# Gated cross-attention with a two-of-eight expert layer: earlier second tile, later weight loads, subtractions on GpSimd, another order of the stacked keys

## The chip, the cores and the metric

The kernel runs on one core of a Trainium2 chip. The metric is the device time of one execution in microseconds; lower is better. The kernel before was timed three times: 310.95, 310.99 and 312.33 us, median 310.99 us. In the text PE is TensorE (PEld its weight loads), DVE is VectorE, ACT is ScalarE, POOL is GpSimd and SP is SyncE.

## The reference

The inputs are `x` (32 batches of 128 tokens by 128 features), `ctx_768` (32 batches of 77 context tokens by 96 features), two gains and the weights. All is float32.

```
q = (layer_norm(layernorm(x)) @ Wq + bq)        16 heads of 8 features
k, v = (layer_norm(ctx) @ Wk + bk), (... @ Wv + bv)
y = softmax(q k^T / sqrt(8)) v                  per batch and head, 128 x 77 scores
x = x + tanh(g_xattn) * y
z = layernorm(x);  logits = z @ w_router;  two experts of eight by top_k, softmax over the two
x = x + tanh(g_ffn) * sum over both of prob * (relu(z @ w1[e])^2 @ w2[e])
```

## The kernel before, in words

**Tiles, steps, slots.** Four batches make a tile, so there are eight tiles (0 to 7). The program is a pipeline of steps i = -2 to 9, and each step has four slots j = 0 to 3. In slot (i, j) each engine works on several batches at once: `near[k]` is the batch k places away from batch j of tile i. A slot has the first two blocks of scores of `near[3]`, the last two of `near[2]`, the turned scores and exponentials of `near[0]` and `near[1]`, the product with the values and the head normalisation of `near[-1]`, and the turn and routing of `near[-2]`. Beside this one slot prepares a later tile (normalise, transpose, project to keys, queries, values) and two experts of an earlier tile run in each slot from (1, 2) on. Each engine's instructions are written in one fixed order, and semaphores join the engines.

**Scores.** The sixteen heads go in four blocks c of four heads. Queries and keys are split into a high part and a low part in fp32r. They are stacked in `qs` and `ks`, 96 rows of three terms with 32 rows each, and 8 rows for the negative maxima. `scores` (L507) makes 128 tokens by 4 x 78 scores in one matmul, so that DVE can take the row maxima (`maximum`, L1043). These maxima are transposed (L513), copied (L753) and sent by DMA into `qs` (L347). `scoresT` (L528) then makes the scores turned with the maximum already subtracted, and ACT takes the exponential (L822).

**How `ks` and `qs` are filled.** ACT writes the high part of the projection (L770, L778) and DVE the low part (L1004, L1013). Then DMAs move 32 partitions of `k_hi` or `k_lo` to 8 partitions of `ks`: twelve DMAs of 39 KB per tile, four on SP (L327) and eight on POOL (L1416, L1421). In `ks` a head's 4 x 78 keys of the four batches lie in one run of 312 numbers. Queries go in three DMAs of 256 KB, all on SP (L341). Tiles 0 and 1 don't do this for queries: `project_query_rows` (L482) makes the stacked rows by four matmuls with `wq_rows`, ACT copies them (L789) and DVE subtracts (L1023).

**Banks.** Short products share two banks of PSUM, `ab_0` and `ab_1`, in a fixed turn (`AB_USES`, `ab_sequence`). A matmul may write a bank only after the one before it has been read out.

**The post chain.** For each batch: product with the values (L551), copy of the heads (L808), transpose (L560), then on DVE reciprocal, product, sum, statistics (L1062 to L1082), then the reciprocal root on POOL (L1388, L1390), the normalisation on DVE (L1088) and the turn on PE (L566) with its two copies on ACT (L814, L815). `low_x` (L1095) on DVE gives the low part of the turned input for the experts. `output` is L596, `hidden` is L589 to L591, `gated` is L1160, `square` is L827.

**Start.** Tile 1 is normalised in slot (-1, 3) and projected in slot (0, 0). Both expert weights are loaded by ACT at (-1, 0) (L842), split or scaled by ACT at (0, 1) to (1, 0) (L849, L853), and the low part of `w1` is made by DVE (L1033). Memsets of `ks` and `vs` for the second parity run on POOL. `keep_on` (L462) issues matmuls whose results nobody reads.

## Time and profile before

| | |
|---|---|
| median of three runs | 310.99 us |
| the profiled execution | 310.82 us, its span 309.0 us, granted clock 0.997 |
| PE busy | 286.2 us, 93% of the span |
| DVE busy | 231.6 us, 75% |
| ACT busy | 179.2 us, 58% |
| POOL busy | 112.4 us, 36% |
| DMA moved | 30.83 MB |

The span is the time from the first to the last instruction on the core; the time of the execution is 1.8 us more. An engine's busy share is an average over the start, the steady middle and the end, which have different limits. A busy PE includes the latency of each matmul, so 93% does not mean that its array works 93% of the time.

### The profile page before, as it was taken

To read this page: it belongs to the slowest core of one execution; us is meant where nothing else is said; L and a number is where in the kernel's file an instruction comes from. 1 tells how busy PE (TensorE), PEld (TensorE's weight loads), DVE (VectorE), ACT (ScalarE), POOL (GpSimd) and SP (SyncE) were. 2 spreads that over 40 slices of the span, in tenths; PEclk is the share of its full clock that TensorE was granted. 3 is DMA by queue.
4 is the path that set the end of the run, shared out by engine and by line. 5 is a ranking of instruction groups with operands and counts; after the bars stand their busy time and mean duration, and the time that the engine had idled before them with its cause. 6 is when DMAs were issued, how large, how long until landed. Compare 5 with 4: busy or idle time off the path is not lost.

```text
span 309.0 us, 7855 instructions
## 1 busy us (share of the span) xinstructions
PE 286.2 (93%) x2837; PEld 235.2 (76%) x2837; DVE 231.6 (75%) x934; ACT 179.2 (58%) x412; POOL 112.4 (36%) x211
## 2 busy tenths in 40 slices
PE   7887889799999999999999999999999999989894
PEld 5555467577878888888888888888788787878784
DVE  7887687788688977888698868886668666646765
ACT  0533656555665676565656665567656555655573
POOL 6594543473156323652166116422612211221110
PEclk9999999999999999999999999999999999999998
DMA  3362301193529363934575275727391620070011
GB/s 71 96 160 59 64 6 51 35 134 110 224 45 118 74 180 139 130 79 127 188 118 101 72 243 76 94 60 249 64 108 35 204 87 3 6 304 6 0 36 34
DMA packets 19078, 30.83 MB, mean 100 GB/s; under 512 B 5321, under 2 KB 11626, under 8 KB 19040
## 3 DMA queue, kind: packets, MB, share of 16 engines
q1 hardware_dynamic: 12144, 22.35, 30.5%
q0 software_dynamic: 3408, 6.61, 9.3%
q10 hardware_dynamic: 3488, 1.38, 1.7%
q8 instruction: 22, 0.36, 0.5%
q14 instruction: 16, 0.13, 0.2%
HBM read 18.94 MB, written 2.21 MB: 68 GB/s over the span
## 4 chain that ended last, share of the span: by engine, by line
PE 56%; DVE 25%; issue 8%; ACT 4%; ACTq 2%; POOL 2%; DMA 1%; SPq 1%; DVEq 0%; POOLq 0%
PE y L596 14%; PE c L551 9%; PE ab L507 6%; DVE u L1160 4%; PE s L528 3%; DVE negm L1043 3%; PE ab L574 3%; PE ab L566 2%; PE h L589 2%; PE h L591 2%; PE h L590 2%; PE ab L457 2%; DVE o L1066 2%; DVE m_parts L1050 2%; DVE st L1078 2%
## 5 line engine op out<-in xcount | busy, mean ns | idle before, releaser
L822 ACT ACTIVATE p<-s 77x512 f32<-77x512 f32 x128 | 74.4, 583 | 18.7 <-PE s L528 18.5
L1043 DVE TENSOR_REDUCE negm<-ab 128x4 f32<-128x308 f32 x128 | 60.4, 474 | 32.6 <-PE ab L507 30.6
L528 PEld LDWEIGHTS s<-qs,ks 104*77 104x77 f32 x512 | 54.0, 148 | 11.6 <-issue 3.7
L596 PE MATMUL y<-w2s,hs 128*128 128x128 f32 x448 | 60.4, 279 | 2.6 <-ACT hs L827 2.6
L528 PE MATMUL s<-qs,ks 104*77 104x128 f32 x512 | 59.2, 238 | 0.6 <-ACT p L822 0.6
L596 PEld LDWEIGHTS y<-w2s,hs 128*128 128x128 f32 x448 | 55.4, 193 | 4.6 <-ACT hs L827 3.7
L1388 POOL TENSOR_SCALAR rs<-mv 128x1 f32<-128x1 f32 x32 | 7.3, 228 | 131.6 <-DVE mv L1082 131.6
L507 PE MATMUL ab<-ks,qs 96*128 96x312 f32 x128 | 49.4, 387 | 4.8 <-DVE negm L1043 1.6
L827 ACT ACTIVATE hs<-u 128x512 f32<-128x512 f32 x56 | 34.9, 624 | 13.6 <-DVE u L1160 13.6
L1160 DVE SCALAR_TENSOR_TENSOR u<-h,gb 128x512 f32<-128x512 f32 x56 | 37.8, 677 | 1.9 <-PE h L591 1.5
L551 PE MATMUL c<-p,vs 77*32 77x128 f32 x1024 | 34.6, 276 | 0.0
L507 PEld LDWEIGHTS ab<-ks,qs 96*128 96x128 f32 x128 | 24.4, 191 | 9.8 <-DVE negm L1043 3.9
L589 PE MATMUL h<-x_hi,w_lo 128*128 128x512 f32 x64 | 31.4, 490 | 0.4 <-DVE top L1104 0.4
L808 ACT ACTIVATE oT<-c 128x256 f32<-128x256 f32 x32 | 12.3, 384 | 32.8 <-PE c L551 32.8
L551 PEld LDWEIGHTS c<-p,vs 77*32 77x32 f32 x1024 | 26.0, 109 | 4.8 <-issue 4.5
L591 PE MATMUL h<-x_hi,w_hi 128*128 128x512 f32 x64 | 25.2, 395 | 0.0
L590 PE MATMUL h<-x_lo,w_hi 128*128 128x512 f32 x64 | 25.2, 394 | 0.0
L1416 POOL DMA_DIRECT2D ks<-k_lo x32 | 18.2, 575 | 16.0 <-issue 8.9
L753 ACT ACTIVATE mT<-ab 32x128 fp32r<-32x128 f32 x32 | 8.4, 263 | 21.8 <-PE ab L513 21.8
L1390 POOL TENSOR_TENSOR rs<-rs,neg_half 128x1 f32<-128x1 f32 x32 | 18.3, 572 | 2.7
L1088 DVE TENSOR_SCALAR xn<-x,mv,rs 128x128 f32<-128x128 f32 x32 | 11.5, 361 | 9.3 <-POOL rs L1390 8.8
L1381 POOL TENSOR_TENSOR nrm<-nrm,neg_half 77x4 f32<-77x4 f32 (+1 forms) x16 | 17.4, 1086 | 1.3
(128 smaller groups left out, 500.6 us busy)
## 6 DMA issues: line engine op xcount, KB each, us to landing
gb<-gates_scratch SPq DMA_DIRECT2D x14, 768.0 KB, 5.7
gb<-gates_scratch SPq DMA_DIRECT2D x14, 256.0 KB, 3.5
qs<-q_hi SPq DMA_DIRECT2D x12, 256.0 KB, 7.6
out_dram<-y_out POOLq DMA_DIRECT2D x7, 256.0 KB, 6.4
x_sb<-in_x_dram POOLq DMA_DIRECT2D x6, 256.0 KB, 3.5
qs<-q_lo SPq DMA_DIRECT2D x6, 256.0 KB, 9.3
ks<-k_hi SPq DMA_DIRECT2D x34, 39.0 KB
ks<-k_lo POOLq DMA_DIRECT2D x32, 39.0 KB, 3.2
```

The costliest lines, as they stand in the source:

```text
L507: nc.tensor.matmul(p[:, 0:J * NP].rearrange("t (i n) -> t i n", n=NP), qs[0:QR, par, c, T * j:T * j + T], ks[0:QR, par, c, :, NP * j:NP * ...
L528: mm = nc.tensor.matmul(p[0:N, T * i:T * i + T], ks[:, par, c, i, NP * j:NP * j + N], qs[:, par, c, T * j:T * j + T], start=True, stop=True)
L551: mm = nc.tensor.matmul(bank_c[VT * i:VT * i + VT, r:r + T], vs[:, par, j, NC * i + c, :], p32[:, m % LR, T * i:T * i + T], start=(c == 0) ...
L589: nc.tensor.matmul(p[:, :], w1_lo[:, e, :], x_hi[:, par, :], start=True, stop=False)
L590: nc.tensor.matmul(p[:, :], w1_hi[:, e, :], x_lo[:, par, :], start=False, stop=False)
L591: nc.tensor.matmul(p[:, :], w1_hi[:, e, :], x_hi[:, par, :], start=False, stop=True).then_inc(h_ready, 1)
L596: mm = nc.tensor.matmul(bank_y[:, D * b:D * b + D], hs[:, e % 2, T * b:T * b + T], w2s[:, e, :], start=(e == 0 and b == 0), stop=(e == E - ...
L822: nc.scalar.activation(p32[:, m % LR, :], src, ACT.Exp).then_inc(p_done, 1)
L827: nc.scalar.activation(hs[:, e % 2, :], u[:, e % 2, :], ACT.Square).then_inc(hs_done, 1)
L1043: nc.vector.tensor_reduce(negm[:, :, c], bank_ab[bank][:, 0:J * NP].rearrange("t (i n) -> t i n", n=NP)[:, :, 0:N], AX.X, ALU.max, negate= ...
L1160: nc.vector.scalar_tensor_tensor(out=u[:, e % 2, :], in0=bank_h[e % 2][:, :], scalar=0.0, in1=gb[:, par, e, :], op0=ALU.max, op1=ALU.mult) ...
L1390: nc.gpsimd.tensor_tensor(rs2[:, 1:2], rs2[:, 0:1], neg_half[:, 0:1], ALU.pow).then_inc(post_p, 1)
```

## The change

Five things are changed together.

- **Order of the stacked keys.** `ks` is now `[row, parity, block, batch, head, 78]` instead of `[row, parity, block, head, batch x 78]`. The matmul of L507 reads one run of 312 numbers instead of four runs of 78. Each DMA into `ks` now writes runs of 78 numbers (312 bytes) where it wrote runs of 312 numbers (1,248 bytes).
- **Tile 1 earlier.** Its normalisation and projections are done in slots (-1, 1), (-1, 2) and (-1, 3). Its queries go the way of all later tiles: one projection, high and low part, DMAs (two on ACT, one on POOL). A table `SIDE` gives nine early uses (value projection of tile 0, and what tiles 1 and 2 need) a bank of their own out of four banks that are idle then.
- **Weights.** `w1` is loaded at (-1, 1) and split by ACT at (-1, 2); `w2` is loaded at (0, 2) and scaled at (1, 0) and (1, 1).
- **Low parts by POOL.** `low_x` of all tiles but the last and the low part of `w1` (in eight pieces) are done by POOL.
- **Order and place of smaller things.** The product with the values stands first on PE in slots (0, 2) to (1, 1). Zeroing of `vs` and part of `ks` is done by ACT (a copy with scale 0) instead of DVE and POOL. Some DMA issues go from ACT or POOL to SP or back. DVE and POOL orders around (0, 0) to (0, 2) differ in detail.

```diff
-AB_MOVED = [(("k", 0), ("ctxT", 0)), (("ctxT", 1), ("mT1", 0)), (("xT", 1), ("s1b2", 0)), (("k", 1), ("s1d2", 0))]
+AB_MOVED = [(("k", 0), ("ctxT", 0))]
+SIDE = {("v", 0): (5, 1), ("ctxT", 1): (2, 1), ("xT", 1): (3, 1), ("k", 1): (4, 1), ("q", 1): (2, 2),
+        ("ctxT", 2): (2, 3), ("xT", 2): (3, 2), ("k", 2): (4, 2), ("q", 2): (2, 4)}
...
-        ks = sb("ks", [MR, 2, NC, J, G * NP], F32R)
+        ks = sb("ks", [MR, 2, NC, G, J, NP], F32R)
...
-        bank_ab = [ps("ab_0"), ps("ab_1")]
+        bank_ab = [ps("ab_0"), ps("ab_1"), bank_h[0], bank_h[1], bank_y, bank_c]
...
-                turned = third if j == (3 if i == -1 else 2) else None
-                made = (1, 1) if (i, j) == (0, 0) else third if j == 3 and i != -1 else None
+                turned = third if j == 2 and i != -1 else None
+                made = third if j == 3 and i != -1 else None
...
-            return 2 if s == 0 else J
+            return {0: 0, 1: J - 1}.get(s, J)
...
-                        if term == 2 and i < k_shared(s):
+                        if term == 2 and (i < k_shared(s) or (s == 0 and i > 0)):
                             continue
                         r = QROWS * term + HD * i
-                        sp.dma_start(ks[r:r + HD, par, :, i, :].bitcast(F32),
-                                     k_hi[QROWS * i:QROWS * i + QROWS].rearrange("p b n -> p (b n)").bitcast(F32))\
+                        sp.dma_start(ks[r:r + HD, par, :, :, i, :].rearrange("p c b n -> p (c b) n").bitcast(F32),
+                                     k_hi[QROWS * i:QROWS * i + QROWS].bitcast(F32))\
                             .then_inc(k_stacked[par], 16)
 
...
+                    if term == 1 and s == 2:
+                        continue
...
+            for i in range(J // 2, J):
+                with nc.allow_non_contiguous_dma(reason="short vectors"):
+                    sp.dma_start(vec[QROWS * i:QROWS * i + QROWS, BQ:BQ + 1],
+                                 bq[QROWS * i:QROWS * i + QROWS].rearrange("(g d o) -> d g o", d=HD,
+                                                                           o=1)).then_inc(bq_in, 16)
+            sp.dma_start(ctx_sb[:, 1], ctx_v[1]).then_inc(ctx_first[1], 16)
+            sp.dma_start(x_sb[:, 1], x_v[1]).then_inc(x_first[1], 16)
...
+                    if (i, j) == (-1, 2):
+                        stack_k(1, 1)
+                    if (i, j) == (0, 0):
                         unit_rows(1)
...
-                nc.tensor.matmul(p[:, 0:J * NP].rearrange("t (i n) -> t i n", n=NP), qs[0:QR, par, c, T * j:T * j + T],
-                                 ks[0:QR, par, c, :, NP * j:NP * j + NP], start=True, stop=True).then_inc(ready, 1)
+                nc.tensor.matmul(p[:, 0:J * NP], qs[0:QR, par, c, T * j:T * j + T],
+                                 ks[0:QR, par, c, j].rearrange("p i n -> p (i n)"), start=True,
+                                 stop=True).then_inc(ready, 1)
...
-                    pe.wait_ge(experts_made, 4)
+                    pe.wait_ge(experts_made, 2)
+                    pe.wait_ge(experts_low, E)
                 if e == 0 and last(s):
-                    pe.wait_ge(late_d, at(LATE, G * s + G - 1, "x_lo"))
+                    pe.wait_ge(low_d, G)
+                if e == 0 and not last(s):
+                    pe.wait_ge(low_p, G * s + G)
...
-                    values_first = i == S - 1 and j != 1
+                    values_first = (i == S - 1 and j != 1) or (i == 0 and j > 1) or (i == 1 and j < 2)
...
+                    if (i, j) == (-1, 2):
+                        project_keys(1)
...
+                    if (i, j) == (-1, 3):
+                        project_queries(1)
...
+            def stack_first_k():
+
+                act.wait_ge(zeroed[0], ZEROED[0])
+                act.wait_ge(hi_k, 1)
+                for i in range(1, J):
+                    r = 2 * QROWS + HD * i
+                    act.dma_start(ks[r:r + HD, 0, :, :, i, :].rearrange("p c b n -> p (c b) n").bitcast(F32),
+                                  k_hi[QROWS * i:QROWS * i + QROWS].bitcast(F32))\
+                        .then_inc(k_stacked[0], 16)
...
+            def stack_q_rows(s, par):
+
+                if s >= 2:
+                    act.wait_ge(s2_ready, NC * G * (s - 1))
+                act.wait_ge(hi_q, s)
+                for term in ((0, 1) if s == 1 else (1,)):
+                    r = QROWS * term
+                    act.dma_start(qs[r:r + QROWS, par].bitcast(F32), q_hi[:, :].bitcast(F32))\
+                        .then_inc(q_stacked[par], 16)
+
+            def clear_some(par, some):
+
+                nc.scalar.activation(vs[:, par, some].rearrange("n b h v -> n (b h v)")
+                                     .rearrange("n (o k) -> n o k", k=D),
+                                     ident[0:N, :].rearrange("n (o k) -> n o k", o=1)
+                                     .broadcast_to([N, (some.stop - some.start) * H * VT // D, D]),
+                                     ACT.Copy, scale=0.0).then_inc(v_ones[par], 1)
+
...
+            act.wait_ge(const_made, 2)
+            for c, half in ((2, 1), (3, 0), (3, 1)):
+                nc.scalar.activation(ks[:, 1, c, 2 * half:2 * half + 2].rearrange("p b i n -> p (b i n)")
+                                     .rearrange("p (o k) -> p o k", k=MR),
+                                     ident[0:MR, 0:MR].rearrange("p (o k) -> p o k", o=1)
+                                     .broadcast_to([MR, 2 * G * NP // MR, MR]),
+                                     ACT.Copy, scale=0.0).then_inc(zeroed[1], 1)
...
-                    if (i, j) == (-1, 0):
-                        load_experts()
+                    if (i, j) == (-1, 1):
+                        clear_some(0, slice(0, G))
+                        evacuate_v(0, 0)
+                        evacuate_ctxT(1)
+                        load_experts(w1_in[:, :, :], w1.rearrange("e c d -> c e d"), first_in)
+                        clear_some(1, slice(0, G // 2))
+                        continue
+                    if (i, j) == (-1, 2):
+                        evacuate_k(1, 1)
+                        max_store(*near[2])
+                        evacuate_xT(1)
+                        prepare_experts(0)
+                        prepare_experts(1)
+                        continue
+                    if (i, j) == (-1, 3):
+                        max_store(*near[2])
+                        evacuate_q(1, 1)
+                        stack_q_rows(1, 1)
+                        clear_some(1, slice(G // 2, G))
+                        exponent(*near[1], 0)
+                        continue
...
+                    if made and made[0] == 2:
+                        stack_q_rows(*made)
...
+                    for part in PREPARING.get((i, j), ()):
+                        prepare_experts(part)
+                    if (i, j) == (0, 2):
+                        load_experts(w2s[:, :, :], w2.rearrange("e d c -> d e c"), experts_in)
...
-            def low_experts():
-
-                for part in range(2):
-                    dve.wait_ge(w1_split, part + 1)
-                    some = slice(E // 2 * part, E // 2 * part + E // 2)
-                    nc.vector.tensor_tensor(w1_lo[:, some, :], w1_in[:, some, :], w1_hi[:, some, :].bitcast(F32),
-                                            ALU.subtract).then_inc(experts_made, 1)
...
-                        clear_values(dve, nc.vector, 0)
...
+                    if (i, j) == (-1, 1):
+                        take(normalise_ctx(1, 1), 2)
+                    if (i, j) == (-1, 2):
+                        normed = normalise_x(1, 1)
+                        take(top_scores)
+                        take(normed)
+                        take(top_scores, 4)
+                        take(normed)
+                        take(tops_of(near[3]))
+                        take(low_keys(1, 1))
...
-                    if near[-2]:
+                    if near[-2] and last(near[-2][0]):
...
+            def low_x(s, par, j):
+
+                bank, k = ab(s, f"turn{j}")
+                pool.wait_ge(ab_taken[bank], k)
+                nc.gpsimd.tensor_tensor(x_lo[:, par, T * j:T * j + T], xT32[:, j % 2, :],
+                                        x_hi[:, par, T * j:T * j + T].bitcast(F32), ALU.subtract).then_inc(low_p, 1)
+
+            def low_expert(e):
+
+                pool.wait_ge(w1_split, 2 * e // E + 1)
+                nc.gpsimd.tensor_tensor(w1_lo[:, e, :], w1_in[:, e, :], w1_hi[:, e, :].bitcast(F32),
+                                        ALU.subtract).then_inc(experts_low, 1)
...
-                    pool.dma_start(ks[r:r + HD, par, :, i, :].bitcast(F32),
-                                   k_lo[QROWS * i:QROWS * i + QROWS].rearrange("p b n -> p (b n)").bitcast(F32))\
+                    pool.dma_start(ks[r:r + HD, par, :, :, i, :].rearrange("p c b n -> p (c b) n").bitcast(F32),
+                                   k_lo[QROWS * i:QROWS * i + QROWS].bitcast(F32))\
...
+            def stack_first_low_q():
+
+                bank, n = ab(1, "q")
+                pool.wait_ge(ab_taken[bank], n)
+                apart(pool)
+                pool.dma_start(qs[2 * QROWS:QR, 1].bitcast(F32), q_lo[:, :].bitcast(F32)).then_inc(q_lo_stacked, 16)
+
+            def zero_keys(c, half):
+
+                nc.gpsimd.memset(ks[:, 1, c, 2 * half:2 * half + 2].bitcast(F32), 0.0).then_inc(zeroed[1], 1)
...
+            zero_keys(0, 0)
+            zero_keys(0, 1)
+            zero_keys(1, 0)
...
             def step(i, par):
                 for j, near, nxt, third, turned, made, ffn in slots(i, par):
                     if (i, j) == (-1, 0):
-                        for c in range(NC):
-                            for half in range(2):
-                                nc.gpsimd.memset(ks[:, 1, c, 2 * half:2 * half + 2].bitcast(F32),
-                                                 0.0).then_inc(zeroed[1], 1)
                         norm_rstd(1, "ctx")
                         norm_rstd(1, "x")
-                    if (i, j) == (-1, 3):
-                        clear_values(pool, nc.gpsimd, 1)
+                        zero_keys(1, 1)
+                        zero_keys(2, 0)
+                        mark_values(pool, nc.gpsimd, 0)
+                    if (i, j) == (-1, 2):
+                        stack_low_k(1, 1)
                     if j == 1 and spread(i - 1):
                         gate_roots(i - 1)
                     if near[-1]:
                         rstd(*near[-1])
+                    if near[-2] and not last(near[-2][0]):
+                        low_x(*near[-2])
                     if j == (1 if i == 0 else 0) and i != -1 and third:
                         norm_rstd(third[0], "ctx")
                         norm_rstd(third[0], "x")
-                    if j == 0 and i > 0 and exists(i + 3):
+                    if j == (1 if i == 1 else 0) and i > 0 and exists(i + 3):
                         load(i + 3, 1 - par)
                     if made:
                         stack_low_k(*made)
-                    if (i, j) in ((-1, 3), (0, 1)):
-                        load(i + 3, 1 - par)
+                    if (i, j) == (0, 0):
+                        mark_values(pool, nc.gpsimd, 1)
+                        stack_first_low_q()
+                        load(2, 0)
+                    if (i, j) == (0, 1):
+                        load(3, 1)
+                    if (i, j) in ((0, 0), (0, 1), (0, 2), (1, 0)):
+                        part = ((0, 0), (0, 1), (0, 2), (1, 0)).index((i, j))
+                        low_expert(2 * part)
+                        low_expert(2 * part + 1)
                     if j == 2 and exists(i - 2) and not last(i - 2):
                         store(i - 2, par)
 
...
```

## Rows read from the trace of the kernel before

**Rows 1.** The page's first line, the span.
```profile
span 309.0 us, 7855 instructions
```

**Rows 2.** Busy time by stretch; columns end with clock, DMA share, GB/s.
```profile
35.84:74.69 38.85, 33.32 (x356) 25.81 (x359) 31.60 (x142) 22.66 (x56) 18.71 (x33) 1.00 0.33 61
90.00:122.75 32.75, 31.98 (x342) 27.24 (x343) 26.57 (x112) 20.70 (x49) 13.60 (x25) 1.00 0.60 127
```

**Rows 3.** Waits in 90:250: waiter, releaser, total us, times, longest.
```profile
PEld ab L566 <- DVE xn L1088: 3.7, 11, 0.5
...
PEld h L578 <- DVE gates L1149: 1.3, 5, 0.3
```

**Rows 4.** ACT and DVE in order of time, slots (0, 0) and (0, 1).
```profile
31.92 0.68 ACT L789 ACTIVATE qs<-c,bq_rows 96x512 fp32r<-96x512 f32 x1
...
35.08 1.06 ACT L822 ACTIVATE p<-s 77x512 f32<-77x512 f32 x2
...
35.48 1.41 DVE L1023 SCALAR_TENSOR_TENSOR qs<-h,bq_rows,qs 32x512 fp32r<-32x512 f32 x2
```

**Rows 5.** One turn of the post chain, slots (0, 2) to (0, 3).
```profile
43.92 0.33 PE L566 MATMUL ab<-ident,xn 128*128 128x128 f32 x1 [1.09 <-DVE xn L1088]
...
44.72 1.08 PE L551 MATMUL c<-p,vs 77*32 77x128 f32 x32
...
46.49 0.41 PE L560 MATMUL c<-ident,oT 128*128 128x128 f32 x2
...
50.03 0.34 DVE L1088 TENSOR_SCALAR xn<-x,mv,rs 128x128 f32<-128x128 f32 x1
...
50.90 0.30 PE L566 MATMUL ab<-ident,xn 128*128 128x128 f32 x1
```

**Rows 6.** DVE in order of time, slot (0, 3).
```profile
53.80 0.68 DVE L1033 TENSOR_TENSOR w_lo<-w_in,w_hi 128x512 fp32r<-128x512 f32 x1
54.40 0.47 DVE L1043 TENSOR_REDUCE negm<-ab 128x4 f32<-128x308 f32 x1
...
55.48 0.28 DVE L1095 TENSOR_TENSOR x_lo<-xT,x_hi 128x128 fp32r<-128x128 f32 x1
55.68 0.28 DVE L1073 TENSOR_TENSOR x<-x_sb,o 128x128 f32<-128x128 f32 x1
```

**Rows 7.** PE waiting for a bank or tile 2's queries, slot (0, 3).
```profile
56.88 1.10 PE L457 MATMUL ab<-xnT,wq 128*128 128x512 f32 x2 [0.80 <-DVE k_lo L1004]
...
72.09 0.38 PE L507 MATMUL ab<-ks,qs 96*128 96x312 f32 x1 [0.18 <-ACT vs L802]
```

**Rows 8.** Around one matmul of the scores, PE and its weight loads.
```profile
125.20 0.19 PEld L507 LDWEIGHTS ab<-ks,qs 96*128 96x128 f32 x1
125.23 0.39 PE L507 MATMUL ab<-ks,qs 96*128 96x312 f32 x1
...
125.46 0.43 PE L528 MATMUL s<-qs,ks 104*77 104x128 f32 x4
```

**Rows 9.** The stretch in which tile 1's twelve key DMAs move alone.
```profile
32.50:38.00 5.50, 4.31 (x48) 2.50 (x46) 3.72 (x6) 3.50 (x7) 4.21 (x8) 1.00 0.45 90
```

**Rows 10.** The page's part 3, the queue with many small loads from DRAM.
```profile
q10 hardware_dynamic: 3488, 1.38, 1.7%
```

**Rows 11.** Tile 7's queries: issue, issue to landing, first matmul that reads.
```profile
223.64 0.59 SPq L341 DMA_DIRECT2D qs<-q_lo  x1
...
qs<-q_lo SPq DMA_DIRECT2D x1, 256.0 KB, 10.3
...
234.80 0.39 PE L507 MATMUL ab<-ks,qs 96*128 96x312 f32 x1
```

**Rows 12.** POOL's power beside DVE's normalisation of the context.
```profile
130.01 1.02 POOL L1381 TENSOR_TENSOR nrm<-nrm,neg_half 77x4 f32<-77x4 f32 x1
...
131.39 1.18 POOL L1381 TENSOR_TENSOR nrm<-nrm,neg_half 128x4 f32<-128x4 f32 x1
131.97 0.56 DVE L982 TENSOR_SCALAR cn<-ctx_sb,c_mv,nrm 77x96 f32<-77x96 f32 x2
```

156 lines of the change are left out of this document (82 added, 74 removed).

## The prediction

> **What bounds the kernel now.** I read the busy time by stretch first. A step of the steady middle lasts 32.75 us, in which PE counts as busy for 31.98 us, DVE for 26.57 us and ACT for 20.70 us [rows 2]. PE bounds this part, and only its short waits can be won. The stretch from the first product with the values to the first slot that has experts lasts 38.85 us for five slots [rows 2], 7.8 us a slot. A steady slot, which has two experts more, takes 32.75/4 = 8.2 us. So the start is bounded by something else than PE's work. Its cause is in the order of time: the turn of the normalised input at 43.92 us is followed by the next one at 50.90 us, 7.0 us later, and between them lie the values at 44.72, the turn of the heads at 46.49 and the normalisation at 50.03 [rows 5]. This loop through all engines sets a slot's length, not any engine's sum. The list of waits in the middle says what PE waits for there: the normalisation (3.7 us in 11 waits over five steps) and the gates (1.3 us) [rows 3], small items of some tenths each.
>
> **Part 1: tile 1's queries, up to the first values at 35.84 us.** ACT makes the stacked rows of tile 1 by four copies from 31.92 us on, and the third and fourth exponentials of the first batch come only at 35.08 us [rows 4]. The values need them. In the changed order ACT copies the queries once (0.7 us, the length of one of the four), issues two DMAs and clears a piece of `vs`, all before the first exponential, which then starts near 30.9 us; three more of about 0.6 us and a small copy give 33.2 us, and the values start near 34.0 us: **-1.8 us**. At the very start ACT gets three zeroing copies (some 0.7 us each, by the 0.68 us of a copy of 512 columns [rows 4]) and issues two DMAs fewer; SP has one DMA of keys fewer in front of the first scores. I take these as equal, with 0.7 us on either side. The moved load of `w1` gives ACT a new wait in slot (-1, 2), behind which the second copy of maxima and the queries stand; it is issued a slot before, and the time above holds 1 us for it. The load of `w2` is issued two slots before its scaling, whose two operations are as many as before, and POOL makes the eight low parts of `w1` in slots in which it waits for DVE: 0 us for these.
>
> **Part 2: slot (0, 1).** DVE subtracts tile 1's rows for 1.41 us from 35.48 us on, with one more of 0.74 us behind it [rows 4], in front of the maxima that PE waits for. After the change that is one subtraction, in slot (0, 0). Then the statistics of tile 2 no longer stand ahead of the post chain: **-2.0 us**; bounds 0 and -3.
>
> **Part 3: the values first, four slots.** In the loop of rows 5 the values (1.08 us) lie between a turn and the turn of the heads that depends on it. Placed before the turn they run while DVE and POOL are on the batch before, and the loop loses about 1.0 us per slot: -4.0 us. In two of these slots DVE's low part of `w1` stands in front of the maxima and the post chain: 53.80 to 54.40 us, 0.6 us from start to start [rows 6]. I count one of them: -0.6 us. The low part of the turned input stands between two operations of the post chain and shifts the next from 55.48 to 55.68 us [rows 6], so 4 x 0.2 = -0.8 us. With banks of their own, the projection of tile 2's queries no longer waits 0.80 us [rows 7]; I count -0.8. Sum -6.2 us. What is late next is tile 2's first score, at 72.09 us [rows 7]: from the projection at 56.88 us to it 15.2 us pass, and shorter slots leave about 12.5 us for copies and DMAs. A tile's query DMA alone takes 10.3 us to land [rows 11]. One of the three DMAs goes from ACT now, but I give back **+1.2 us**: -5.0 us.
>
> **Part 4: the low part off DVE in the rest.** 24 batches have slots with experts and get their low part from POOL. DVE has 0.2 us less in each. PE waits for the normalisation or the gates in about half the slots (16 waits of these two in 20 slots [rows 3], some of them for the same reason): 12 x 0.2 = **-2.4 us**; bounds 0 and -4.8. On POOL the subtraction costs between the 0.28 us that DVE takes [rows 6] and the 1.02 us of its own longest arithmetic [rows 12]; I take 0.45 us, nearer to DVE's, since the 1.02 us is a power. POOL waits for DVE's statistics most of the time, which hides it. It stands behind the reciprocal root and in front of tile preparation, where it delays the context's normalisation once per step by 0.45 us; a row maximum waits behind that, with 0.6 us of slack. Uncovered it would cost 0.45 x 5 = 2.3 us.
>
> **Part 5: the layout of the keys, PE's side.** The weights of L507 start to load at 125.20 us, the matmul at 125.23 us, and the next group starts at 125.46 us [rows 8]. 312 columns and one exposed load of weights in 0.26 us leave nothing that reading four runs could have cost beyond a few cycles. I take 0; the bound is 128 x 0.02 = -2.6 us.
>
> **Part 6: the layout of the keys, the DMA's side.** Twelve key DMAs move alone in 5.5 us at a share of 0.45 [rows 9]: 2.48 us of all 16 engines. A DMA has 8 rows by 4 runs, so 384 runs of 1,248 bytes take 2.48 x 16 / 384 = 103 ns each. After the change there are 1,536 runs of 312 bytes. Priced by bytes a run costs 26 ns, by number 103 ns; the queue with small loads from DRAM has 3,488 packets in 1.7% of 16 x 309 us, 24 ns each [rows 1, 10]. I take 40 ns, near the small packets: 3.84 us, 1.36 us more per tile. The slack is small: tile 7's last query DMA is issued at 223.64 us, lands 10.3 us later at 233.94 us, and PE reads at 234.80 us [rows 11], 0.86 us. So 0.5 us stall for each of five tiles: **+2.5 us**; bounds 0 and 5 x (9.9 - 2.48 - 0.86) = +32.8 us. POOL's and SP's issue times I leave as they are; POOL has about 2 us of slack behind its eight issues.
>
> **Sum.** -1.8 - 2.0 - 5.0 - 2.4 + 0 + 2.5 = -8.7 us. The profiled execution took 310.82 us (span 309.0 us and 1.8 us around it), 0.17 us from the median of 310.99 us, so the sum holds for the median: **302.3 us**, own range 299 to 306 us.
>
> **Rivals.**
> - *The short runs are dear (slower side).* Every tile's keys and queries share the 16 engines in the same window, and PE stands at the first score of a tile. The gain without part 6 is 11.2 us, or 2.2 us per tile of five; it is gone when the key DMAs need 2.48 + 0.86 + 2.2 = 5.6 us, 58 ns a run. At 70 ns: 6.72 - 3.34 = 3.4 us a tile, 16.9 us in all, 316.7 us. For it speaks that slack is under 1 us; against it, that small packets elsewhere cost 24 ns.
> - *A run costs twice its bytes.* 52 ns a run gives 5.0 us, 1.65 us of stall per tile, 8.3 us: 308.1 us. The Trainium skill, page "DMA: Bandwidth & Descriptors", section "Specifications", says that below 512 bytes a transfer does a read-modify-write; the new runs have 312 bytes, the old ones 1,248. No row here shows such a doubling; the 24 ns of small packets [rows 10] are loads from DRAM and don't exclude it.
> - *POOL's subtraction holds up the normalisation.* It starts right behind the reciprocal root, when DVE's normalisation starts too. If that waited for its end, it would be 0.35 us late, and PE waits for it in two slots of three: 19 x 0.35 = 6.6 us, 308.9 us. For it: the power beside DVE's operation took 1.18 us instead of 1.02 us. Against it: DVE's operation started and ended as usual, 0.56 us, inside POOL's [rows 12]. The Trainium skill, page "SBUF — State Buffer", section "SBUF: two separate sides", says that the port pair shared by the two is an exclusive lock held for a whole instruction; the rows show at most 0.16 us, on POOL.
> - *ACT is the new bound up to slot (0, 1).* Its zeroing, DMA issues and the wait for `w1` in slot (-1, 2), 3 to 4 us in all, stand in front of the first exponentials. Parts 1 and 2 then give nothing: 306.1 us.
> - *More cover than counted.* Part 6 costs nothing and the middle recovers twice part 4: 297.4 us.
>
> **How the numbers follow.** Forecast 0.48; short runs dear 0.12; doubled 0.09; POOL 0.08; ACT 0.12; more cover 0.11. A measurement of this kernel tells 0.5% (1.6 us) from no change. Faster takes the forecast, ACT and more cover (0.71), most of doubled (0.06) and half of POOL (0.04): 0.81. Same takes 0.03 and 0.03 of these two: 0.06. Slower 0.13. The range 297 to 312 us holds all but the dear runs and a little of either end.
>
> **What would show it.** Right: from the first values to the first slot with experts about 32 us instead of 38.85; the first values near 34 us; PE's wait for the normalisation smaller in the middle; a step there 32.5 to 33 us, with a wait of 0.5 us for a DMA in front of L507. L507's mean stays near 390 ns. Wrong: a wait of over 2 us for `ks` or `qs` at each tile's first score (part 6); L1088 over 0.5 us or starting late behind POOL (part 4); first values at 36 us or later (part 1). The forecast falls if steps in the middle get longer than 34.2 us.

## The result, and the profile after

The changed kernel takes **333.56 us** (median of 4 runs, 330.56 to 338.58) against 311.60 us for the kernel before on the same chip: a ratio of **1.062** (95% interval 1.058 to 1.067), slower. Two of the four runs (336.05 and 338.58 us) were executions in a slower state at a lower clock, so the ratio compares the other two (331.07 and 330.56 us), as every ratio below does. The prediction said 302.3 us, range 297 to 312. Its profiled execution took 331.07 us, with a span of 329.3 us.

First the changed kernel's page: the span, the clock that TensorE was granted in 40 slices, the DMA packets by size, the queues (packets, MB, share of 16 engines' span), and the chain that ended last.

```profile
span 329.3 us, 7846 instructions
...
PE 288.0 (87%) x2827; PEld 241.8 (73%) x2827; DVE 224.5 (68%) x898; ACT 181.8 (55%) x415; POOL 128.9 (39%) x243
...
PEclk9998559999999999997999879999999999999998
...
DMA packets 24159, 31.64 MB, mean 96 GB/s; under 512 B 10785, under 2 KB 16410, under 8 KB 24120
...
q1 hardware_dynamic: 15536, 22.08, 34.0%
q0 software_dynamic: 4336, 6.77, 13.4%
...
PE 45%; DMA 26%; DVE 11%; POOL 7%; issue 5%; ACT 3%; ACTq 1%; SPq 1%; DVEq 0%; POOLq 0%
```

The span grew by 20.3 us [rows 1], while PE's busy time is 288.0 us and DVE's 224.5: no engine has that much more to do (POOL has 16.5 us more, and is busy for 39%). DMA is now 26% of the chain that ended last, where it was 1%. The list of waits (waiter, releaser, total us, times, longest) names what:

```profile
PE ab L523 <- DMA ks<-k_hi: 16.7, 6, 3.6
PE s L545 <- DMA qs<-mT: 6.6, 1, 6.6
```

L523 is the matmul of the scores (L507 before), L545 the transposed scores (L528), L568 the values (L551), L583 the turn of the normalised input (L566), L465 the projection of keys. Six times PE stands at a tile's first score for its keys, for 2.1 to 3.6 us; and once, in the start, for the small transfer of the maxima (16 KB). In order of time, start of the first values, of the projection of keys for tiles 2 to 7, and the span (us), in the four kernels that matter most here:

| | values | tile 2 | 3 | 4 | 5 | 6 | 7 | span |
|---|---|---|---|---|---|---|---|---|
| before | 35.84 | 54.10 | 84.59 | 117.31 | 150.07 | 182.83 | 215.68 | 309.0 |
| changed | 44.43 | 62.87 | 95.08 | 129.29 | 166.04 | 203.51 | 235.92 | 329.3 |
| e1 (changed, old key layout) | 37.30 | 56.90 | 87.20 | 119.72 | 152.44 | 184.92 | 217.38 | 309.2 |
| e11 (e1, queries later, filled) | 34.19 | 50.35 | 80.32 | 112.85 | 145.57 | 178.05 | 210.50 | 302.2 |

Steps of the changed kernel in the view by stretch, columns as in [rows 2]:

```profile
95.08:129.29 34.21, 31.52 (x343) 27.20 (x342) 26.00 (x108) 20.49 (x50) 16.04 (x28) 1.00 0.65 111
129.29:166.04 36.75, 33.20 (x343) 28.64 (x342) 26.21 (x108) 20.62 (x50) 16.05 (x28) 0.95 0.66 114
166.04:203.51 37.47, 34.41 (x344) 29.85 (x342) 26.01 (x108) 20.61 (x50) 16.05 (x28) 0.91 0.63 108
203.51:235.92 32.41, 31.82 (x343) 27.22 (x342) 26.13 (x108) 20.54 (x50) 14.48 (x26) 1.00 0.55 118
```

Two things are to be seen. PE waits (in the first row it is busy 31.5 of 34.2 us at full clock), and then its clock falls (0.95, 0.91), so that its own work gets longer. The table shows where the loss lies. Against e1, 7.1 us of its 20.1 us have come before the first values, and most of the rest in the three steps from 95.08 to 203.51 us. And the last row has neither: 32.41 us, less than before's 32.75 [rows 2]. It is the step in which no ctx and x are loaded any more.

### The profile page after: what moved, and what is told of

Its sections match the earlier page's. It is cut to its first block, busy times and chain, and to the rows that moved or that the text cites. A ratio compares the mean times of both kernels' runs of the same rounds, so it can differ in the third digit from the quotient of the medians.

```text
span 329.3 us, 7846 instructions
## 1 busy us (share of the span) xinstructions
PE 288.0 (87%) x2827; PEld 241.8 (73%) x2827; DVE 224.5 (68%) x898; ACT 181.8 (55%) x415; POOL 128.9 (39%) x243
## 4 chain that ended last, share of the span: by engine, by line
PE 45%; DMA 26%; DVE 11%; POOL 7%; issue 5%; ACT 3%; ACTq 1%; SPq 1%; DVEq 0%; POOLq 0%
DMA ks<-k_hi 21%; PE y L616 10%; PE c L568 6%; PE ab L523 5%; PE s L545 4%; POOL ks L1520 4%; DMA qs<-mT 3%; POOL ks L1525 2%; DVE u L1239 2%; DVE negm L1122 2%; PE h L609 2%; PE h L611 2%; PE h L610 2%; PE ab L591 2%; PE ab L473 1%
## 5 line engine op out<-in xcount | busy, mean ns | idle before, releaser
L545 PEld LDWEIGHTS s<-qs,ks 104*77 104x77 f32 x512 | 55.0, 152 | 19.6 <-DMA qs<-mT 7.0
L545 PE MATMUL s<-qs,ks 104*77 104x128 f32 x512 | 60.1, 242 | 9.1 <-DMA qs<-mT 6.6
L523 PE MATMUL ab<-ks,qs 96*128 96x312 f32 x128 | 50.1, 398 | 18.6 <-DMA ks<-k_hi 16.7
L616 PE MATMUL y<-w2s,hs 128*128 128x128 f32 x448 | 63.2, 287 | 1.4 <-ACT hs L882 1.4
L616 PEld LDWEIGHTS y<-w2s,hs 128*128 128x128 f32 x448 | 57.8, 200 | 3.6 <-ACT hs L882 2.6
L523 PEld LDWEIGHTS ab<-ks,qs 96*128 96x128 f32 x128 | 25.6, 202 | 22.7 <-issue 14.5
L882 ACT ACTIVATE hs<-u 128x512 f32<-128x512 f32 x56 | 34.9, 623 | 11.2 <-DVE u L1239 10.6
L568 PE MATMUL c<-p,vs 77*32 77x128 f32 x1024 | 36.1, 284 | 0.0
L568 PEld LDWEIGHTS c<-p,vs 77*32 77x32 f32 x1024 | 27.1, 113 | 5.9 <-issue 5.1
L1520 POOL DMA_DIRECT2D ks<-k_lo x32 | 21.1, 697 | 18.8 <-issue 13.3
L1525 POOL DMA_DIRECT2D ks<-k_hi x27 | 18.2, 850 | 0.0
L1167 DVE TENSOR_SCALAR xn<-x,mv,rs 128x128 f32<-128x128 f32 x32 | 12.9, 404 | 7.2 <-POOL rs L1481 6.8
## 6 DMA issues: line engine op xcount, KB each, us to landing
qs<-q_lo SPq DMA_DIRECT2D x6, 256.0 KB, 12.4
```

Source lines behind the costliest of these rows:

```text
L523: nc.tensor.matmul(p[:, 0:J * NP], qs[0:QR, par, c, T * j:T * j + T], ks[0:QR, par, c, j].rearrange("p i n -> p (i n)"), start=True, stop= ...
L545: mm = nc.tensor.matmul(p[0:N, T * i:T * i + T], ks[:, par, c, j, i, 0:N], qs[:, par, c, T * j:T * j + T], start=True, stop=True)
L568: mm = nc.tensor.matmul(bank_c[VT * i:VT * i + VT, r:r + T], vs[:, par, j, NC * i + c, :], p32[:, m % LR, T * i:T * i + T], start=(c == 0) ...
L616: mm = nc.tensor.matmul(bank_y[:, D * b:D * b + D], hs[:, e % 2, T * b:T * b + T], w2s[:, e, :], start=(e == 0 and b == 0), stop=(e == E - ...
L882: nc.scalar.activation(hs[:, e % 2, :], u[:, e % 2, :], ACT.Square).then_inc(hs_done, 1)
L1520: pool.dma_start(ks[r:r + HD, par, :, :, i, :].rearrange("p c b n -> p (c b) n").bitcast(F32), k_lo[QROWS * i:QROWS * i + QROWS].bitcast(F ...
```

## The experiments

e1 to e4 ran together, then e5 to e8, e9 and e10, e11 and e12, e13 to e16, e17 and e18; each ratio is to the kernel before in the same batch.

**e1: the changed kernel with the old layout of the keys.**
```
-        ks = sb("ks", [MR, 2, NC, G, J, NP], F32R)
+        ks = sb("ks", [MR, 2, NC, J, G * NP], F32R)
```
(with the same for the copies, `k_hi` and `k_lo` as one run of `(b n)`, and for the readers)

> The changed kernel with the old order of the keys alone put back: DMAs into ks write runs of 1,248 bytes again, everything else stays changed. Theory A (the short runs are the loss, the rest of the change gains what was predicted): the 16.7 us and 6.6 us that PE waits for DMAs go, the clock stays at 1.0, and the time is 311.6 - 11 = 300 us, 297 to 304. Theory B (the rest of the change loses too: the start, POOL's subtractions, DMA issues on ACT): 315 to 325 us, slower than the kernel before.

310.18 us, ratio 0.995 (0.992 to 0.997): not the 297 to 304 us of theory A, nor a loss as in theory B. Its waits for the same two transfers:

```profile
PE s L544 <- DMA qs<-mT: 4.3, 1, 4.3
PE ab L523 <- DMA ks<-k_hi: 1.8, 2, 1.0
```

That is 6.1 us where the changed kernel waits 23.3, and PE's busy time is 283.6 us for 288.0. So the loss by the layout is 17.2 us of waits and 4.4 us of work that took longer.

**e2: the kernel before with the new layout and nothing else** (the edit the other way round).

> The kernel before with the new order of the keys alone. Theory A: each tile's last key or query DMA lands 2 to 4 us later, PE stands 1.5 to 3 us at six to seven first scores and is slowed after some of these by a lower clock: 325 to 338 us. Theory B: under 316 us. L507 stays at a mean of 385 to 400 ns in both, if reading four runs never cost PE anything; if it did, its mean falls to 350 ns or less.

331.02 us, ratio 1.061 (1.057 to 1.066). With e1 this settles where the loss is: in the layout, which costs 6.1% (19 to 20 us) on the kernel before and nearly 7% (21 us) within the changed one. The rest of the change, forecast to bring 11.2 us, brought 0.5% (1.6 us).

**e3: the changed kernel with runs of two blocks** (624 bytes: `ks = sb("ks", [MR, 2, NC, G // 2, J, 2 * NP], F32R)`).

> The changed kernel with the keys of two batches side by side: DMAs into ks write runs of 624 bytes, twice as many as of old and half as many as now. If each run costs the same whatever its size, the added load is a third of that of the 312-byte runs: 1.4 us more of all engines per tile, PE waits 0.5 to 1 us per tile, and the time is 4 to 8 us over that with the old order. If the cost comes with runs under 512 bytes only, it is within 1.5 us of that with the old order.

315.65 us, from 311.17 to 317.84, too scattered for a ratio (5.5 us over e1 by the medians). The queues q1 and q0 say more than the time. The share times 16 times the span is 2,033 us in e1 (15,472 packets), 2,271 us in e3 (17,568) and 2,497 us in the changed kernel (19,872). e1's two queues on its page:

```profile
q1 hardware_dynamic: 12080, 22.08, 30.3%
q0 software_dynamic: 3392, 6.75, 10.8%
```

The same of e3:

```profile
q1 hardware_dynamic: 13232, 22.08, 33.1%
q0 software_dynamic: 4336, 6.76, 12.3%
```

The copies into `ks` write 3,040 runs in these two queues in e1, twice as many in e3 and four times as many in the changed kernel. A further run takes 78 ns of engine time going from 1,248 to 624 bytes and 37 ns from 624 to 312, though the bytes are the same; both prices hold what the runs do to the packets beside them. On q1 alone, which has one packet more for each further run, they are 136 and 59 ns. So a run gets no dearer below 512 bytes. The rule of the Trainium skill that the prediction cited (page "DMA: Bandwidth & Descriptors", section "Specifications", a read-modify-write below 512 bytes) would have made the second step the dear one; the trace doesn't agree with it as the cause here. The time does grow more in the second step (310.2, 315.7 and about 331 us). A slack that is used up first would look like that, but no run separates it.

**e4: the kernel before with the values first in the four slots.**
```
-                    values_first = i == S - 1 and j != 1
+                    values_first = (i == S - 1 and j != 1) or (i == 0 and j > 1) or (i == 1 and j < 2)
```


> The kernel before with one edit: the product with the values stands first on PE in slots (0, 2) to (1, 1). By the prediction the loop through turn, heads and normalisation loses 1.0 us in each of four slots: 4 us less, 307.6 us, 306 to 309. Rival: another wait (DVE's order or a bank) takes its place and it gives under 1 us.

311.95 us, ratio 1.002 (1.001 to 1.004): none of the 4 us, as its rival said.

**e5: e1 with the three copies of tile 1's queries later**
```
                         evacuate_q(1, 1)
-                        stack_q_rows(1, 1)
...
                     if near[0]:
                         exponent(*near[0], 3)
+                    if (i, j) == (0, 0):
+                        stack_q_rows(1, 1)
...
                 pool.wait_ge(ab_taken[bank], n)
+                pool.wait_ge(p_done, NC)
```
(and `stack_first_low_q` behind `load(2, 0)` and the low parts). Its reason is the start of e1. In PE's order of time PE waits there, and the stretch behind shows the clock (columns as in [rows 2]):

```profile
35.96 0.78 PE L544 MATMUL s<-qs,ks 104*77 104x128 f32 x4 [4.30 <-DMA qs<-mT]
...
30.00:45.00 15.00, 10.21 (x75) 8.55 (x76) 4.76 (x21) 5.22 (x12) 4.94 (x11) 0.57 0.72 80
```

> The changed kernel with the old layout of the keys (e1), and the three copies of tile 1's queries (256 KB each) issued after the exponentials of tile 0's first slot instead of before its last preparing slot. If it was these copies that held the small transfer of the maxima for 4.30 us in e1, and the idle PE that lowered the granted clock to 0.57 between 30 and 45 us: first values at 33.0 to 34.0 us (e1 37.30), no wait over 1.5 us for qs<-mT, mean clock back at 0.99, time 304 to 306.5 us. Rival, the keys' copies or SyncE's own order in front of that transfer are what is late: the wait stays over 3 us, the time within 1 us of e1's 310.2.

306.89 us, ratio 0.984 (0.981 to 0.986). First values at 33.85 us, and the wait is 2.31 us instead of 4.30. That the clock would recover was wrong. What PE did and was granted in e5:

```profile
30.00:32.00 2.00, 0.20 (x2) 0.00 (x0) 0.54 (x2) 1.00 (x3) 1.99 (x4) 1.00 0.74 123
32.00:34.00 2.00, 1.49 (x10) 1.17 (x14) 0.30 (x1) 0.59 (x1) 0.23 (x1) 0.51 0.94 244
34.00:36.00 2.00, 2.00 (x33) 1.52 (x30) 0.56 (x2) 0.15 (x1) 0.00 (x0) 0.50 1.11 188
...
40.00:42.00 2.00, 2.00 (x11) 1.54 (x10) 0.37 (x2) 0.74 (x4) 1.22 (x3) 0.50 0.02 8
42.00:44.00 2.00, 2.00 (x40) 1.63 (x39) 1.26 (x5) 1.07 (x2) 0.00 (x0) 0.93 0.06 16
```

TensorE is idle for 1.8 of 2 us, and then works for 10 us at 0.50, that is 1.2 GHz instead of 2.4. (The profiled execution took 310.26 us, 3.4 us more than the median.)

**e6: e1 with the subtraction of `x_lo` back on VectorE.**

> e1 with the subtraction of x_lo back on VectorE for all tiles. By the prediction's part 4 this costs 0.6 us a step in the four middle steps, 2.4 us in all: 312.6. Rival: TensorE is 98% busy in the middle steps of either kernel and they differ by only 0.1 to 0.3 us between before and e1, so that the subtraction stood on no path that ends last: 0 to 1 us, 310.2 to 311.2.

310.98 us, ratio 0.997 (0.993 to 1.000), beside e1's 310.18: 0 to 1 us, where part 4 had 2.4.

**e7: the changed kernel, its copies in long runs to wrong places.**
```
-    ks[r:r + HD, par, :, :, i, :].rearrange("p c b n -> p (c b) n").bitcast(F32)
+    ks[r:r + HD, par].rearrange("p c b i n -> p c (b i n)")[:, :, G*NP*i:G*NP*i + G*NP].bitcast(F32)
```


> The changed kernel, its keys' layout and every reader of it as they are, but the copies write their 1,248 bytes a row in one run each, to wrong places among a row's blocks and heads (the scores are not the reference's). Bytes and number of instructions are the changed kernel's; only the number of runs falls to a quarter. If the runs alone are the loss: 310 to 311 us, as e1. If the readers of the new layout (TensorE's moving operand, the narrower weights) have a part: more than 312, and 333 if they are all of it.

310.84 us, ratio 0.998 (0.995 to 1.001). All readers work in the new layout, and the loss is gone: it is the runs of the keys' copies and not the readers. The matmul of the scores in the new layout:

```profile
L523 PE MATMUL ab<-ks,qs 96*128 96x312 f32 x128 | 48.8, 387 | 3.9 <-DMA ks<-k_hi 2.0 <-DVE negm L1122 1.2 <-ACT mT L781 0.4
```

**e8: e5 without the values first** (e4's line undone).

> e5 with the values of a head no longer put first in the slots (0,2) to (1,1). By the prediction's part 3 (1.0 us in each of four slots) this is 4.0 us slower than e5. By what e4 showed on the kernel before (0.2% the other way), it is within 0.7 us of e5.

308.47 us, ratio 0.990 (0.986 to 0.994): 1.6 us slower than e5, with intervals that all but meet (e5's ends at 0.986), and short of the 4 us.

**e9 and e10: what is left of the wait in e5.** In e9 the copies are issued behind the exponential that itself waits for the maxima (`pool.wait_ge(p_done, NC + 1)`, and ACT's at the end of the slot); in e10 `load(2, 0)` too.

> e5 with the three query copies of tile 1 issued one exponential later still: behind the exponential that itself waits for the small transfer, so that nothing of them can be in front of it (in e5 two of them were issued at 30.05 and 30.73 us, beside it, and 2.31 us of wait were left). If the copies still made that wait: it goes, first values at 31.6 to 32.5 us (e5 33.85), 304 to 305.5 us. Rival, the loads of tile 2's ctx and x at 29.19 and 29.95 us are what stands in front: the wait stays at about 2 us and the time at 306.9. Against both: tile 1's first scores (44.9 us in e5) come to wait for the copies, over 1 us for qs<-q_lo, and the time is 307 or more.

> e9 with the loads of tile 2's ctx and x (371 KB) also put behind that exponential, after the query copies. If the loads were in front of the small transfer: its wait is under 0.5 us, first values at 31.6 us or sooner, 303.5 to 305 us. If the query copies alone were: as e9 within 0.5 us. Against it: tile 2's statistics come late and DVE with them, over 1 us of wait for ctx_sb or x_sb.

308.07 us (0.989, 0.983 to 0.994) and 309.56 us (0.991, 0.988 to 0.994): no better than e5. In e9 the wait stays 2.26 us, so that the copies had no part in what e5 left; in e10 it is 1.51 us: the loads are some 0.8 us of it, and 1.5 us is left with neither in front. Both missed on the time.

**e11: e5 with the wait filled.**
```
                         scores(*near[3], 0)
+                    if (i, j) == (0, 0):
+                        keep_on(bank_h[1], 8)
```


> e5 with 8 matmuls of the identity by itself (no result is used; four of the kind take 1.03 us in e5) put in front of the wait for the maxima's transfer, where e5's TensorE is idle for 2.31 us and its granted clock then stands at 0.50 to 0.51 from 32 to 42 us although TensorE is busy all of that time. If the idle time is what lowers the clock: it stays at 1.00 from 30 to 45 us, the 10 us at half clock shrink by 3 to 5 us, and the time is 302 to 304.5 us. Rival, the clock falls there whatever TensorE does in those 2 us: 0.66 for 30 to 45 us again and 306.5 to 307.5 us.

304.89 us, ratio 0.980 (0.978 to 0.983). The calls are 16 matmuls in the trace and longer than I had read (3.62 us), so that they start from the last score and end 0.8 us past e5's wait; the clock stays full:

```profile
30.04 3.62 PE L478 MATMUL h<-ident 128*128 128x256 f32 x16
...
30.00:45.00 15.00, 13.91 (x145) 11.68 (x145) 9.77 (x44) 6.65 (x16) 7.54 (x14) 1.00 0.49 96
```

In e5 these 15 us were granted 0.66. The mean clock is 0.992 to 1.000 in e11's six runs and never over 0.986 in e5's. The idle time was the cause of the lower clock. What that cost is less sure: 2.0 us by the two medians, 1.0 us by the two ratios, whose intervals overlap, and the time is a little above the 302 to 304.5 us expected.

**e12: e1 filled with 16 calls.**

> e1 (queries' copies where the change has them) with 16 such matmuls in the same place, for its wait of 4.30 us. The copies still hold the transfer, so that first values stay at 37 to 37.5 us; if idle time lowers the clock, it stays at 1.00 and the time falls by the price of some 10 us at half clock alone, to 305.5 to 307.5 us. If the clock isn't it: 310 us as e1.

314.96 us, ratio 1.009 (1.006 to 1.013): too much filling. The filling ran from 32.14 to 41.65 us, 5.7 us past the transfer, and the clock had already fallen in front of it, at 30 us, behind a wait of 1.82 us for the exponentials. It says nothing against e11, and nothing for it.

**e13 and e16: 5 calls instead of 8; and e13 without the values first.**

> e11 with 5 calls of the filling product for 8 (in e11 the 8 lasted 3.62 us, from 30.04 on, where the wait to be covered was 2.31 us). If they only have to cover the wait: the clock stays at 1.00 between 30 and 45 us, first values at 32.9 to 33.5 us (e11 34.19), and 303.3 to 304.3 us. If the longer filling was needed to hold the clock: it falls again and the time is 306 or more.

> e13 with the values of a head no longer put first in (0,2) to (1,1). Prediction's part 3: 4.0 us slower than e13. By e8 against e5 (308.47 and 306.89, where low clocks blur it) 1.6 us; by e4 nothing. I expect 0.5 to 1.5 us slower than e13.

304.92 us (0.978, 0.974 to 0.982) and 307.02 us (0.983, 0.978 to 0.988). e13's first values start at 33.40 us, but its clock is 0.92 from 30 to 45 us (full behind the covered wait, lower from 42 us on), and it comes out as e11. The values first are worth 1.6 us by the ratios and 2.1 us by the medians with the start mended, about half of the forecast.

**e14 and e15: the short runs with e11's start, and with filling in front of the wait for keys.**
```
+                p, ready = claim(s, f"s1{'abcd'[c]}{j}")
                 if j == 0 and c == 0:
+                    if s > 0:
+                        keep_on(p, 6)
                     stacked(s, par)
```


> The changed kernel with its short runs of the keys, and with e11's two edits (queries' copies later, 8 filling calls). If the loss by the runs is one of the later tiles (keys landing too late for each tile's first scores) it stays: e11's 304.9 plus 17 to 21, 322 to 326 us. If much of it was the start's wait (6.63 us for the maxima in the changed kernel, and the clock behind it): 312 to 318 us.

> e14 with 6 more filling calls (some 2.7 us) in front of the wait for the keys at the first scores of tiles 1 to 7, into the bank that these scores are about to write. Where the keys are waited for, the filling takes no time; what it changes is that TensorE isn't idle. If a part of the loss is the lower granted clock behind these waits (in the changed kernel 0.95 over the span, against 0.977 in e1): mean clock 0.98 or more and 5 to 9 us less than e14. If it is the waits alone: as e14, or up to 5 us more where there was no wait to fill.

335.74 us (1.072, 1.067 to 1.077) and 330.44 us (1.050, 1.044 to 1.057). e14 missed both forecasts: with the mended start the short runs cost some 29 us (1.072 against e11's 0.980). The first values come earlier, at 41.30 us instead of 44.43, but PE now also waits for the queries' low part (qs<-q_lo), 5.6 us in two waits that the changed kernel doesn't have. e15: the mean clock rises from between 0.93 and 0.96 to 0.97 and more, and 5.3 us (medians) to 6.8 us (ratios) come back although the filling also runs where there is little to wait for. So the lower clock is about a fifth to a quarter of the loss by the runs, and the waits the rest; the 4.4 us of longer work out of 20 us against e1 say the same.

**e17 and e18: the loads of ctx and x two slots later.**
```
-                    if j == (1 if i == 1 else 0) and i > 0 and exists(i + 3):
+                    if j == 2 and i > 0 and exists(i + 3):
                         load(i + 3, 1 - par)
```
Its reason is how long the same copies take alone and in company. First the kernel before, then e2, over the stretch in which tile 1's twelve copies of keys move with almost nothing beside them:

```profile
32.00:38.00 6.00, 4.81 (x49) 2.67 (x47) 3.72 (x6) 4.00 (x7) 4.33 (x8) 1.00 0.41 83
```
```profile
37.00:44.50 7.50, 6.18 (x64) 4.15 (x63) 5.55 (x18) 4.67 (x9) 5.09 (x8) 1.00 0.54 67
```

The last but one column is the DMA share: 6.0 x 0.41 = 2.5 us of 16 engines before, 7.5 x 0.54 = 4.05 us with short runs, which is 42 ns a run. In company it is another matter. A whole step of e1:

```profile
87.20:119.72 32.52, 31.89 (x344) 27.28 (x342) 26.14 (x108) 20.55 (x50) 15.27 (x28) 1.00 0.53 117
```

It takes 0.53 x 32.52 = 17.2 us of the engines in e1, and 0.65 x 34.21 = 22.2 us in the changed kernel, 5.0 us more; in its step without loads 0.55 x 32.41 = 17.8 us, against 16.9 us in e1's. The keys' high parts, over all tiles, from issue to landing (before, then changed):

```profile
ks<-k_hi POOLq DMA_DIRECT2D x30, 39.0 KB, 5.8
```
```profile
ks<-k_hi POOLq DMA_DIRECT2D x27, 39.0 KB, 10.7
```

> The changed kernel, short runs of the keys and all, with the loads of ctx and x for the tile after next (371 KB a step, on GpSimd's queue behind the keys) issued in a step's third slot instead of its first (second in step 1). In the changed kernel the steps from 95.08 and 129.29 us, which have these loads, last 34.21 and 36.75 us, and the keys' high parts land 11.6 us after their issue; the step from 203.51 us, which has none, lasts 32.41 us, and they land after 7.9 us. If the short runs are dear only where they meet these loads: steps of 32.5 to 33.5 us, and 318 to 323 us in all. If they are dear by themselves or beside the queries' copies: within 3 us of the changed kernel's 333.6.

> e13 (long runs) with the same move of the loads. The keys are waited for only 1.9 us in all there, in two waits of at most 1.0 us, so the move can't give much: 303.9 to 304.9 us (e13 304.92). If the loads held back the keys in every step with long runs too: under 303.

327.45 us (1.047, 1.041 to 1.053) and 304.47 us (0.978, 0.974 to 0.983). Neither theory of e17 holds alone. Meeting the loads costs some 5 of the 21 us (1.047 against 1.062); the other 16 stay. Some 7 of these are the loss in front of the first values, which the edit doesn't touch: they come at 45.19 us in e17. e18 is e13 again within the scatter, so the move itself is worth nothing with long runs.

**The best version** is e11, e13 or e18, which can't be told apart: 304.5 to 304.9 us, 2.0 to 2.2% under the kernel before and nearly 8% under the changed one by the ratios.

## Why the prediction was wrong

**Part 6, the layout on the DMA's side, is the step that failed.** It is the term that set the sign: +2.5 us forecast, 19 to 21 us measured. Its price of a run was good: 40 ns forecast, 42 ns measured, for copies that move alone. What failed is the sentence behind it, that 1.36 us more of all engines per tile meet a slack of 0.86 us and leave 0.5 us of stall. That adds up engine time as if the keys had the engines to themselves. They move together with 768 KB of queries and 371 KB of loads; in that company the engines spend 5 us more a step, the high parts land 4.9 us later, and PE waits 2.1 to 3.6 us in six places. Over the whole span the 9,120 further runs of the two queues took 464 us of engine time, 51 ns each: 3.6 us of all engines a tile, where the forecast had 1.36 and the copies alone show some 1.6. Even this, with the prediction's slack and its five tiles, makes only (3.6 - 0.86) x 5 = 13.7 us. The sum had no term for the start, where 7.1 us were lost against e1: PE waits 3.62 us instead of 0.96 for tile 0's keys and 6.63 us instead of 4.30 for the maxima. The evidence was in [rows 11]: a copy that takes 10.3 us to land for 256 KB was not moving alone, and [rows 9], from which the slack's other side was taken, is the one stretch in which keys do. The slack of 0.86 us is that of tile 7, beside which no loads move any more. The rival "the short runs are dear" had the mechanism and most of the place, at 12% and 316.7 us. The 3.6 us a tile lie between its 4.2 us (70 ns a run) and the 2.5 us of the rival at 52 ns; both left out the start and the clock.

A second price stood nowhere in the prediction: **the clock**. Of the seven waits of over 2 us in the changed kernel, those that end at 22.10, 43.09, 151.60 and 187.79 us are followed by work at a lowered clock (it had fallen in front of the second of these already, at 34 us), those that end at 83.00, 116.44 and 257.13 us by work at 1.00. The mean granted clock is 0.95 in the changed kernel; e15 puts this at 5 us or more.

**Part 1, first values at 34.0 us.** They came at 44.43 us, and at 37.30 us with long runs (e1). The working counted two DMAs that ACT issues and their time on ACT; it did not follow the 256 KB that each of them moves. Issued at 27.55 us, they and the low part's keep the DMA engines full while the 16 KB of maxima have to pass: 4.30 us of wait. With the copies issued later and the wait filled the values start at 34.19 us (e11) or 33.40 us (e13): the term's size was right, the transfers it moved were not priced.

**Parts 2 and 3, -7.0 us between the first values and the first slot with experts.** In e11 this stretch lasts 69.83 - 34.19 = 35.64 us instead of 38.85 [rows 2]: -3.2 us, less than half. Part 2 gave about half of its 2.0 us: from the first values to the first turn of the normalised input it was 8.08 us and is 6.93. (From values to values 8.88 us became 5.92, but there the values' own move in front of the turn is counted too: in e16, without it, it is 8.04.) The turns of the normalised input, 6.98, 9.33 and 6.39 us apart before ([rows 5] has the first), are 7.35, 7.03 and 6.74 us apart in e11. So the slot with w1's low part and the keys' bank gained 2.3 us, and the two others lost 0.4 each. The 1.0 us a slot for the values first fails by its premise, that they would run while DVE and POOL are still on the batch before. In e11's DVE, in order of time:

```profile
47.12 0.39 DVE L1169 TENSOR_SCALAR xn<-x,mv,rs 128x128 f32<-128x128 f32 x1
```

and in its PE:

```profile
47.46 1.08 PE L567 MATMUL c<-p,vs 77*32 77x128 f32 x32
48.47 0.33 PE L582 MATMUL ab<-ident,xn 128*128 128x128 f32 x1
```

PE gets to the values only when the normalised input is ready, and the turn now stands behind them. PE is busy 31.83 of the 35.64 us: the loop was no longer the only bound. e16 gives 1.6 to 2.1 us for all four slots, e4 nothing on the kernel before.

**Part 4, -2.4 us in the middle.** From the end of that stretch to the end of the span it is 234.3 us before and 232.4 in e11, -1.9 us, but little of it is the subtraction: e6 leaves 0 to 1 us. On POOL it takes 452 ns, as assumed (0.45 us). It is not without effect on DVE, though. Where the normalisation starts within the subtraction, it ends 0.07 us or more behind it, as here in e1:

```profile
60.05 0.46 POOL L1486 TENSOR_TENSOR x_lo<-xT,x_hi 128x128 fp32r<-128x128 f32 x1
60.12 0.47 DVE L1166 TENSOR_SCALAR xn<-x,mv,rs 128x128 f32<-128x128 f32 x1 [1.12 <-POOL rs L1480]
```

17 of the 32 normalisations last 0.47 or 0.48 us in e1, 4 do in the kernel before, and 4 last 0.46 to 0.48 us in e6, where the subtraction is back on DVE; the usual length is 0.34 or 0.35 us. So the rival that POOL's subtraction holds up the normalisation had a true mechanism, but 0.13 us instead of 0.35 and no price that shows: e6 isn't faster, and PE and its weight loads wait for the normalisation for 6.5 us in e1, 6.1 us in e6 and 9.2 us before. The forecast 6.6 us of loss is refuted. The lock that the Trainium skill's page "SBUF — State Buffer" states (section "SBUF: two separate sides") would hold the normalisation until the subtraction ends. The trace agrees in this, that none of those overlapping ended before it.

**Part 5, 0 us on PE's side.** Right: 387 ns in e7 and 387 ns before.

**ACT as the new bound.** Not as stated. But one sentence of it, DMA issues in front of the first exponentials, is e1's 1.82 us of wait for them, which e5 brought down to 0.3 us.

Without part 6 the prediction would have said 299.8 us for e1, which took 310.2; e11 reached 304.9 us. That e1 lies within 297 to 312 us is owed to the width of the range, since 1.6 us of the 11.2 came.

## What to carry to other kernels

A copy's cost is to be read in the company in which it moves: price it in the busiest stretch that it will share, and take the slack from the same stretch, not from one where it is alone. Whoever moves a DMA earlier has to ask which small transfer on the path now lands behind it. And a new wait of PE can have a second price, the clock behind it; a few matmuls without use, issued in the wait, can win some of it back.

## What the runs showed of the hardware

- A copy within the chip's memory costs by its runs and not only by its bytes. With the same bytes in runs of 1,248, 624 or 312 bytes all that moved in the two queues took 2,033, 2,271 and 2,497 us of engine time (e1, e3, changed), 78 and then 37 ns for each further run. Twelve copies that move alone took 2.5 and 4.05 us of 16 engines (before, e2).
- The number of packets is not the number of runs on every queue. Eight copies of keys by GpSimd's queue (tile 1's, before and e2) went from 256 packets to 384 with a fourfold number of runs, and that queue's time from 10.1% to 15.8% of 15 us. Why, no run tells.
- TensorE's clock fell to 0.50 behind 1.8 us idle of 2 (e5, from 32 us) and stayed there some 10 us, with TensorE busy. In the kernel before 1.3 idle of 2 us (24 to 26 us) left it at 1.00, and in the changed kernel a wait of 3.42 us (to 83.00 us) did too. So the length of one wait doesn't decide it in these traces.
- A DVE operation of 0.34 us that starts some 0.06 us into a GpSimd operation of 0.45 us lasts 0.47 us and ends 0.08 us behind it (e1, the normalisation beside the subtraction of `x_lo`).

Open: what makes the rest of e17's loss, some 9 us when the start is taken off. The queries' copies share the window with the keys and land later too (q_lo 12.4 us, before 9.3), but no run took them away.
